# One-hot operands of the pair-count matmuls stored pair by pair in a graph attention kernel on Trainium2

## The reference

```python
h  = relu(layernorm(x))                                  # x: 12500 x 128, src, dst: 400000
att = sigmoid(h[src] @ W_att[:d] + h[dst] @ W_att[d:] + b_att)
aggregated = segment_sum((h[src] @ W_msg + b_msg) * att, dst)
gi = aggregated @ W_ih.T + b_ih;   gh = h @ W_hh.T + b_hh
r = sigmoid(i_r + h_r);  z = sigmoid(i_z + h_z);  n = tanh(i_n + r * h_n)
h_new = (1 - z) * n + z * h
out = x + gamma * (h_new - mean(h_new)) * rsqrt(var(h_new) + eps) + beta   # over the nodes
```

## Time and profile before

| | |
|---|---|
| median of 3 runs | 2611.94 us (2603.95 to 2614.46) |
| profiled execution | 2611.86 us, its span 2608.8 us |
| busy: PE, weight loads | 2263.1 us (87%), 2056.7 us (79%) |
| busy: DVE, ACT, POOL | 1904.7 (73%), 1888.2 (72%), 1902.6 us (73%) |
| mean granted TensorE clock | 0.887 of full speed |

### The profile page before, as it was taken

How to read it: one execution, slowest core, us unless ns; L and a number is a source line. 1 busy time by engine, 2 the same in 40 slices (tenths; PEclk the granted TensorE clock), 3 DMA queues, 4 the chain that set the end, 5 groups by cost and what they waited for, 6 DMA issues and landing times.

```text
span 2608.8 us, 51662 instructions
## 1 busy us (share of the span) xinstructions
PE 2263.1 (87%) x16757; PEld 2056.7 (79%) x16757; DVE 1904.7 (73%) x4599; ACT 1888.2 (72%) x6472; POOL 1902.6 (73%) x1864
## 2 busy tenths in 40 slices
PE   2435999899999999899998999899998999989984
PEld 2434888888888888888888888788887888888884
DVE  4765677778777777777777777778777777777744
ACT  1248788868877788778787787868777788868533
POOL 3736777777777777777777777777777777777770
PEclk9665899989998999989998999989998899989986
DMA  7852222222222222222222222232222222222246
GB/s 123 228 142 48 59 61 61 59 63 60 59 60 65 58 61 60 59 63 59 59 59 62 61 61 59 58 65 60 58 59 59 62 62 59 59 63 57 59 110 193
DMA packets 207016, 188.41 MB, mean 72 GB/s; under 512 B 105097, under 2 KB 172859, under 8 KB 206619
## 3 DMA queue, kind: packets, MB, share of 16 engines
q0 software_dynamic: 59136, 122.10, 21.1%
q1 hardware_dynamic: 147610, 63.01, 10.4%
HBM read 158.86 MB, written 26.10 MB: 71 GB/s over the span
## 4 chain that ended last, share of the span: by engine, by line
PE 55%; DMA 13%; POOL 12%; ACT 7%; issue 6%; DVE 5%; SPq 2%; DVEq 0%; ACTq 0%; POOLq 0%
PE ps L1379 28%; DMA row_ring<-node_table,set_idx 12%; PE ps L1374 11%; POOL row_ring L721 10%; PE ps L1363 9%; ACT big L836 4%; PE ps L1386 2%; PE ps L1385 2%; ACT gate_ring L832 2%; DVE gate_ring L1112 1%; PE ps L1387 1%; PE ps L1388 1%; POOL big L716 1%; POOL big L702 1%; SPq L423 1%
## 5 line engine op out<-in xcount | busy, mean ns | idle before, releaser
L721 POOL DMA_INDIRECT row_ring<-node_table,set_idx x1760 | 1808.5, 1028 | 583.5 <-issue 389.8
L836 ACT ACTIVATE big<-set_score,big 128x128 f32<-128x128 f32 x4214 | 1361.6, 389 | 4.7 <-DMA set_score<-dst_scores 4.3
L1379 PE MATMUL ps<-big 128*128 128x128 f32 x8428 | 1240.3, 284 | 0.0
L1379 PEld LDWEIGHTS ps<-big 128*128 128x128 f32 x8428 | 1114.3, 197 | 31.1
L832 ACT ACTIVATE gate_ring<-set_win,row_ring 128x64 f32<-128x64 f32 x1760 | 593.8, 341 | 543.5 <-DMA row_ring<-node_table,set_idx 502.2
L1112 DVE SCALAR_TENSOR_TENSOR gate_ring<-lane,set_rel,gate_ring 128x64 f32<-128x64 f32 x1760 | 494.9, 282 | 580.3 <-ACT gate_ring L832 565.1
L1363 PE MATMUL ps<-gate_ring,row_ring 128*128 128x64 f32 x3520 | 687.3, 281 | 207.2 <-DVE gate_ring L1112 204.6
L1363 PEld LDWEIGHTS ps<-gate_ring,row_ring 128*128 128x128 f32 x3520 | 587.3, 210 | 287.1 <-DVE gate_ring L1112 240.8
L1129 DVE TENSOR_TENSOR big<-ps,big 128x784 f32<-128x784 f32 x688 | 665.5, 967 | 0.6 <-PE ps L1374 0.6
L1374 PE MATMUL ps<-key_hot,lo_hot 128*128 128x196 bf16 x2752 | 604.7, 355 | 0.0
L1374 PEld LDWEIGHTS ps<-key_hot,lo_hot 128*128 128x128 bf16 x2752 | 323.8, 128 | 80.0
(11 more groups left out here) (116 smaller groups left out, 995.9 us busy)
## 6 DMA issues: line engine op xcount, KB each, us to landing
row_ring<-node_table,set_idx POOLq DMA_INDIRECT x1760
big<-in_x_dram SPq DMA_DIRECT2D x48, 256.0 KB, 8.3
node_table<-big SPq DMA_DIRECT2D x24, 258.0 KB
hT_spill<-big SPq DMA_DIRECT2D x24, 256.0 KB, 6.2
out_dram<-big SPq DMA_DIRECT2D x24, 256.0 KB
set_win<-dst_scores SPq DMA_DIRECT2D x176, 32.0 KB
h_blk<-hT_spill SPq DMA_DIRECT2D x87, 40.0 KB
set_score<-dst_scores SPq DMA_DIRECT2D x43, 64.0 KB, 2.9
```

Source lines behind the costliest of these rows:

```text
L721: nc.gpsimd.indirect_dma_start(row_ring[:, i % ROWS_RING, :], None, table, bass.IndirectOffsetOnAxis(ap=set_idx[:, par, i:i + 1], axis=0)) ...
L836: return nc.scalar.activation(a_buf[par][:, h, :], set_score[:, score, :], ACT.Sigmoid, bias=m_all[:, h, D:ROW])
L1379: return nc.tensor.matmul(ps[:, AM_BANK, 0:P], m_all[:, h, 0:D], a_buf[1 - par][:, h, :], start=h == 0, stop=h == HI - 1)
```

## The change

`lo_hot` and `key_hot` are laid out with the pair outermost, so that each pair's one-hots are contiguous: 128 values of `lo_hot` as weights, 196 values of `key_hot` as moving operand. For this `lane_lo` loses its doubling, and `lo_hots` compares each lane with one value that is repeated 128 times (`unsqueeze(2).broadcast_to`), where it compared lanes in twos with two adjacent values. `key_hots` keeps its innermost dimension of two adjacent values in both inputs. Numbers of instructions, elements, waits and results are as before.

```diff
-        lane_lo = sb("lane_lo", [P, P, 2], BF16)
+        lane_lo = sb("lane_lo", [P, P], BF16)
-        lo_hot = sb("lo_hot", [P, 2, BATCH // 2, P, 2], BF16)
-        key_hot = sb("key_hot", [P, 2, HI, BATCH, 2], BF16)
+        lo_hot = sb("lo_hot", [P, 2, BATCH, P], BF16)
+        key_hot = sb("key_hot", [P, 2, BATCH, HI, 2], BF16)
-            nc.gpsimd.iota(lane_lo[:, :, :], [[1, P], [0, 2]], base=0, channel_multiplier=0,
+            nc.gpsimd.iota(lane_lo[:, :], [[1, P]], base=0, channel_multiplier=0,
             def lo_hots(b, s, first):
                 nc.vector.tensor_tensor(
-                    lo_hot[:, b, :, :, :], lane_lo[:, :, :].unsqueeze(1).broadcast_to((P, BATCH // 2, P, 2)),
-                    set_lo[:, s, first:first + BATCH].rearrange("p (j w) -> p j w", w=2).unsqueeze(2).broadcast_to(
-                        (P, BATCH // 2, P, 2)), ALU.is_equal)
+                    lo_hot[:, b, :, :], lane_lo[:, :].unsqueeze(1).broadcast_to((P, BATCH, P)),
+                    set_lo[:, s, first:first + BATCH].unsqueeze(2).broadcast_to((P, BATCH, P)), ALU.is_equal)
             def key_hots(b, s, first):
                 nc.vector.tensor_tensor(
                     key_hot[:, b, :, :, :],
-                    lane_key[:, :].rearrange("p (h w) -> p h w", w=2).unsqueeze(2).broadcast_to((P, HI, BATCH, 2)),
-                    set_key[:, s, first:first + 2 * BATCH].rearrange("p (j w) -> p j w", w=2).unsqueeze(1).broadcast_to(
-                        (P, HI, BATCH, 2)), ALU.is_equal).then_inc(hots_ready, 1)
+                    lane_key[:, :].rearrange("p (h w) -> p h w", w=2).unsqueeze(1).broadcast_to((P, BATCH, HI, 2)),
+                    set_key[:, s, first:first + 2 * BATCH].rearrange("p (j w) -> p j w", w=2).unsqueeze(2).broadcast_to(
+                        (P, BATCH, HI, 2)), ALU.is_equal).then_inc(hots_ready, 1)
-                    last = nc.tensor.matmul(ps_pairs(q, j), lo_hot[:, b, t // 2, :, t % 2], key_hot[:, b, :, t, :],
+                    last = nc.tensor.matmul(ps_pairs(q, j), lo_hot[:, b, t, :], key_hot[:, b, t, :, :],
```

## The result

| | before | changed |
|---|---|---|
| median | 2607.5 us (2598.8 to 2616.12, 11 runs) | 2626.92 us (2616.05 to 2633.2, 11 runs) |
| ratio | | 1.0076, 95% interval 1.0062 to 1.0091 |
| span of the profiled execution | 2608.8 us | 2623.5 us |

The account below looks back on a forecast made before the run. POOL's gathers and gaps were taken to set the time, with PE's 165 us saving hidden. The profiled 2611.86 us plus 45 us of net holds (0.13 us over 344 beats) gave 2657 us; range 2608 to 2710, chance 0.73.

Parts of the forecast that it names:

- What bounds the kernel: Main stage: POOL's gathers and gaps, 1808.5 + 546.6 = 2355.1 us, set the time; PE follows and delays no gather.
- The 0.305 us gaps: POOL before its gathers: the gap left when it waits for nothing; PE releases falling into it delay nothing.
- TensorE: Count matmuls in `build`: 0.115 us each instead of 0.175, 165 us less PE time, bounds 0 and 241, hidden by POOL.
- The low compare: `lo_hots` on DVE: from 0.686 to 1.218 us each, 183 us more DVE time over 344 beats.
- the prediction's rival: Main-stage gathers: "Nothing moves the end", 2612 us, here because a `tensor_tensor` would not hold up descriptor writing; chance 0.13.
- The hold and the give-back: POOL under compares, shown beat: loses 0.53 us under `lo_hots`, regains 0.40 under `key_hots`, net 0.13.
- forecast's arithmetic over all 329 beats: Beats from 300 to 2500 us at their old starts, nothing carried on: mean loss 0.159 us, or 55 us.
- the shown beat's 45: One worked main-stage beat: net loss 0.13 us, 45 us over 344 beats, taken between 22 and 55.
- its formula: POOL's gathers: one that starts under a compare with two SBUF inputs ends 0.82 us after that compare ends.
- a DVE load of 81%: Main stage: DVE busy time goes from 1757 to 1940 of some 2400 us, costing nothing while its backlog stays small.
- Its 22 us for evenly spread starts: Main-stage beats: total loss if the compares' positions behind gather starts spread evenly, against 55 us at old starts.
- A gather that has started first is not held.: POOL's gathers: only one that starts under a two-SBUF-input compare is held; no size given.

Follow-up runs that it names:

- Experiment 1: Changed kernel's contiguous layouts, but low numbers stored twice so the low compare reads pairs; against the kernel before: 2611.23 us, ratio 1.0002.
- experiment 4: Changed kernel with low and key compares both replaced by one-input reductions, one-hots left out, timing only; against the kernel before: 2469.36 us, ratio 0.9474.
- e6: The changed kernel itself run again, beside e5_third; ratio to the kernel before 1.0089.
- e7: The changed kernel itself run once more, later; ratio to the kernel before 1.0106.
- e3: Changed kernel with the low compare replaced by an equally long one-input reduction, low one-hots left out, timing only; against the kernel before: 2576.85 us, ratio 0.9875.
- e1: Contiguous layouts with low numbers stored twice, so the low compare is quick again; against the kernel before: 2611.23 us, ratio 1.0002.
- e5_third: New lo_hot with slow low compare, old interleaved key_hot; third run, kernel before at 2609.45 us: 2628.25 us, ratio 1.0073.
- e2: Kernel before, old layouts, with the low compare's walk turned so one value is repeated (1311 ns); against the kernel before: 2643.75 us, ratio 1.0147.
- v1: Experiment 1's kernel with low compare cut in 2 and key compare in 4, pieces together; third run 2565.72 us, ratio 0.9844; 1.003 and 1.0027 on slow chips.
- e5_key_old: Same kernel as e5_third (new lo_hot, old key_hot), first run, on a chip where the kernel before takes 3002.47 us: ratio 1.0032.
- v2: Changed kernel's layouts, low compare as 8 tensor_scalar instructions, key compare cut into 4; where the kernel before takes 3002 us: ratio 1.0071.
- v3: Like v1, but 8 key compares and 4 low ones; where the kernel before takes 3002 us: ratio 1.0083.

## Why the prediction was right in kind and wrong in size

**What bounds the kernel: right.** The 0.305 us gaps were the proof. Experiment 1 shows it from PE's side and experiment 4 from POOL's.

**TensorE: right in effect, off in size.** I took 0.115 us a count matmul; it is 0.085 at the upper clock level, half the old spacing and the far bound, and 0.165 at the lower. With the mean spacings that is 2,752 x 0.079 = 217 us less, not 165. It was hidden, as said.

**The low compare: right.** 1.218 us forecast, 1.220 measured. The low compares' own time rose by 184 us, as reckoned, and the busy time of DVE as a whole by 160. The rule in the Trainium skill (Vector Engine (DVE) Microarchitecture Reference, section 5.1), that a two-input instruction which reads one element again and again gives one result a cycle and not two, agrees with this trace: 1,024 results in 1.220 us against 0.686. What the prediction's rival made of the Trainium skill's inference in SBUF — State Buffer ("Who interferes with whom"), that a `tensor_tensor` does not hold up GpSimd's writing of DMA descriptors and so costs these gathers nothing, does not agree: the gather of 527.57 took 1.54 us. No run tells which part of a gather's work is held; a gather also reads its indices (`set_idx`) from SBUF.

**The hold and the give-back: right.** What each gather takes beyond 0.944 us, summed over the timelines from 300 to 2500 us and divided by the beats. A gather counts to the compare under which it starts (or at most 0.02 us ahead of it):

| held, us a beat | by low compares | by key compares | change |
|---|---|---|---|
| before | 33.5/329 = 0.10 | 99.4/329 = 0.30 | |
| forecast's arithmetic over all 329 beats | +0.43 | -0.27 | +0.16 |
| changed | 138.9/327 = 0.42 | 10.7/327 = 0.03 | +0.32, -0.27: +0.05 |
| changed, second profile (e6) | 146.0/326 = 0.45 | 10.8/326 = 0.03 | +0.35, -0.27: +0.08 |
| changed, third profile (e7) | 142.5/327 = 0.44 | 8.4/327 = 0.03 | +0.33, -0.28: +0.06 |
| e3 (slow, one SBUF input) | 0.4/329 = 0.00 | 101.9/329 = 0.31 | -0.10, +0.01: -0.09 |

The give-back has the size that was worked out. **The step that failed** is the next one, as the prediction put it: "The positions will shift with the longer gathers, so I take the shown beat's 45, between the two." The mis-sized term is the loss under the low compare, +0.43 us a beat reckoned at the old starts, +0.32 measured (0.35 and 0.33 in the other two profiles). The net of 0.054 us times 344 beats is 18 us, against the 45 that were taken.

The starts moved more than the prediction let them. By its formula, a compare of 1.218 us that starts x us behind a gather's start holds the next gather for 1.218 - (1.249 - x) + 0.82 - 0.944 = x - 0.155 us, so the mean start decides. Starts of the low compare, counted by how long after a gather's start they come (the few beyond 1.2 us are left out), and their mean:

| us behind the gather's start | 0-0.2 | 0.2-0.4 | 0.4-0.6 | 0.6-0.8 | 0.8-1.0 | 1.0-1.2 | mean | masks that waited for ACT |
|---|---|---|---|---|---|---|---|---|
| before | 29 | 31 | 32 | 137 | 59 | 38 | 0.68 | 669 |
| e1 (quick compare, fast PE) | 30 | 42 | 14 | 146 | 56 | 38 | 0.67 | 665 |
| changed | 58 | 51 | 43 | 96 | 35 | 39 | 0.58 | 451 |
| changed, second profile (e6) | 41 | 58 | 41 | 111 | 32 | 41 | 0.59 | 458 |
| changed, third profile (e7) | 59 | 41 | 37 | 116 | 43 | 28 | 0.58 | 436 |
| e5_third (slow compare, old PE) | 65 | 45 | 48 | 92 | 44 | 32 | 0.56 | 428 |
| e2 (slower still, old PE) | 59 | 50 | 47 | 104 | 32 | 31 | 0.56 | 427 |
| e3 (slow, but holds nothing) | 56 | 52 | 23 | 90 | 53 | 52 | 0.61 | 413 |

The last column is from the view of waits; the lines of before and changed are:

```profile
DVE gate_ring L1112 <- ACT gate_ring L832: 565.1, 669, 21.5
```

```profile
DVE gate_ring L1111 <- ACT gate_ring L832: 425.5, 451, 21.0
```

Whenever the low compare takes 1.2 us or more, the starts come earlier behind the gathers and fewer masks wait for ACT. PE's pace has no part in it (e5). The holds by the low compare are not needed for it either, though without them the move is smaller (0.61 in e3). My reading is this. With a quick compare, DVE is often ahead and waits for the gate of a gather, so its compares start at a fixed time behind gathers, mostly 0.6 to 0.8 us, where a long low compare would catch the next gather early. With a slow one, DVE works more often from its backlog (instructions whose inputs are ready already), and a compare starts where the backlog has brought it. The counts agree with that; no experiment set DVE's backlog by itself, so this last link is argued and not shown.

The prediction let the starts change only as far as the gathers do, and took its value near the arithmetic at old starts, although it had itself worked out a DVE load of 81%, which is what came (1917.7 of 2373.1 us). Its 22 us for evenly spread starts lie near the measured 20, but by luck. The starts are not even: 96 to 116 lie between 0.6 and 0.8 us, where an even spread over 1.249 us would put 52. And by the formula above even starts give a loss of 0.48 us under the low compare, so 0.48 + 0.03 - 0.40 = 0.11 us a beat or some 37 us, and not 22.

One sentence of the prediction is too strong: "A gather that has started first is not held." In the trace of before, 10 gathers that started under a mask and at most 0.11 us ahead of a compare were held to 0.82 us behind that compare's end. The longest of all, 1.907 us, is one of them; a start under the key compare could give 0.97 + 0.82 = 1.79 at most. v1's long holds are of the same kind.

## What to carry to other kernels

Ask the engine that does nothing but issue whether its gaps are ever longer than their least: 1,758 gaps of 0.305 us showed the bound that busy shares and the chain hid. On such a kernel, what matters about a VectorE instruction is how many SBUF inputs it has and how long it lasts, since a gather of GpSimd that starts under a compare with two SBUF inputs waited for its end; cut it, keep the pieces apart, or store an operand twice so that it is read in pairs. When the cost depends on where one engine's instructions meet another's, the starts of before are one case only: here a slower compare moved the mean start by some 0.1 us, and of the 0.16 us a beat reckoned at the old starts, half to two thirds were gone.

## What the runs showed of the hardware that was not expected

- A gather can be held through a whole run of two-input instructions that follow without a gap (2.11 us in v1); more often it is released at the end of the one under which it started (103 against 35 in v1_third).
- The masks have two SBUF inputs too, but with 0.28 us they hold hardly anything: of 568 gathers in the changed kernel that started under a mask with no compare near, 11 took more than 0.99 us, the longest 1.06.
- The same kernel takes 2609 to 2611 us on some chips (3, 9 and 11 of those used) and 2999 to 3002 us on others (0, 5 and 14). There, gathers do wait, as the view of waits of e5_key_old shows (us, times, longest; "remote" is the profile's own word for a releaser and is not explained further):

```profile
POOL row_ring L721 <- issue: 412.1, 1327, 2.9
...
DVE big L1128 <- remote: 248.8, 169, 6.1
...
POOL row_ring L721 <- PE ps L1362: 207.1, 280, 11.2
POOL row_ring L721 <- remote: 189.1, 152, 2.6
...
PE ps L1362 <- issue: 129.2, 143, 6.2
```

  POOL's gaps come to 808 us in e5_key_old against 547 in e5_third, and PE stands in "issue", waiting for nothing that the profile shows. The preparation stage of the same kernel is longer too (245.7 us against 187.0), and its mean granted clock is 0.857 against 0.889. All variants of the compares are 0.2 to 0.8% slower than the kernel before there, and those with most instructions are the slowest (v2 and v3, 55,102 instructions; v1 53,038; 51,662 before). What holds PE up on those chips stays open.
- A bf16 moving operand read as adjacent twos, 32 bytes apart, streams at half the pace of a contiguous one at the upper clock level (0.175 against 0.085 us for 196 columns) and at nearly the same pace at the lower (0.18 against 0.165). Weights at a step of two elements cost nothing that could be seen beside such an interleaved operand (355 ns before, 354 in e5_third with contiguous weights); no run has them beside a contiguous one.
